# One tile more between the scores and the values of a causal attention, with a fourth buffer

## The reference

```python
xn = layernorm(x)
s = attn(xn, H=16, causal)        # Dh = 64: softmax(q k^T / 8, causal) v, then Wo, then layernorm
nodes = {-1: xn}
for c in range(6):                # a graph of 6 nodes
    q = ew[c,0] * (nodes[c-1] @ We[eq]);  k = ew[c,1] * (nodes[snode] @ We[ek])
    v = ew[c,2] * (nodes[snode + nsrc//2] @ We[ev])
    nodes[c] = act_w[c] * mha(q, k, v, H=8) + q      # Dh = 128, not causal
g = silu(layernorm(nodes[5]))
out = x + s * g
```

## Time and profile before

| what | value |
|---|---|
| runs shown | 8005.43 and 8122.02 us, median 8063.72 us |
| the profiled execution's own time | 7821.7 us |
| its span (slowest core, core 5) | 7820.2 us |
| spans of the 8 cores | 7784.9 to 7820.2 us |
| mean granted TensorE clock of the cores | 0.844 to 0.847 |
| PE busy, whole span | 5836.1 us (75%) |
| ACT busy | 2739.9 us (35%) |
| DVE busy | 2197.2 us (28%) |

### The profile page before, as it was taken

How to read it: one execution, slowest core, us unless ns; L and a number is a source line. 1 busy time by engine, 2 the same in 40 slices (tenths; PEclk the granted TensorE clock), 3 DMA queues, 4 the chain that set the end, 5 groups by cost and what they waited for, 6 DMA issues and landing times.

```text
span 7820.2 us, 62342 instructions; the slowest of 8 cores (7784.9 to 7820.2 us)
## 1 busy us (share of the span) xinstructions
PE 5836.1 (75%) x21827; PEld 1920.4 (25%) x21827; DVE 2197.2 (28%) x3068; ACT 2739.9 (35%) x2612; POOL 364.9 (5%) x354
## 2 busy tenths in 40 slices
PE   0677787777987779877789777897777878778830
PEld 0222233222332223322234222342222311111110
DVE  3133321333213332133321333213332122222155
ACT  0155432544215543155421455214552123333301
POOL 0100011000110001100011000110000100000000
PEclk9989998898998989989999888998888955566655
DMA  2300042000420004300033000230003200000013
GB/s 74 105 1 0 1 108 65 1 1 20 116 80 1 1 10 111 95 1 1 1 81 113 0 1 1 81 105 9 1 0 83 63 0 0 0 0 0 2 44 105
DMA packets 204568, 289.37 MB, mean 37 GB/s; under 512 B 141576, under 2 KB 141800, under 8 KB 204268
## 3 DMA queue, kind: packets, MB, share of 16 engines
q1 hardware_dynamic: 204236, 285.39, 12.7%
q0 software_dynamic: 32, 0.00, 0.0%
HBM read 218.24 MB, written 33.55 MB: 32 GB/s over the span
## 4 chain that ended last, share of the span: by engine, by line
PE 67%; DVE 18%; issue 6%; DMA 4%; ACT 4%; SPq 1%; DVEq 1%; POOL 0%; ACTq 0%; POOLq 0%
PE ps L384 17%; PE ps L564 9%; PE ps L869 8%; DVE attb L615 6%; PE ps L625 6%; PE ps L634 5%; PE ps L447 5%; PE ps L610 5%; DVE stat L515 4%; PE ps L508 3%; PE ps L595 3%; PE ps L586 3%; DVE attb L499 2%; DMA fio<-x 2%; ACT attb L675 1%
## 5 line engine op out<-in xcount | busy, mean ns | idle before, releaser
L675 ACT ACTIVATE attb<-ps,negM,scal 128x1024 bf16<-128x1024 f32 x1536 | 1770.0, 1201 | 1928.3 <-DVE negM L531 1432.9
L384 PE MATMUL ps<-slot,wbuf 128*128 128x512 bf16 x6144 | 1376.1, 385 | 227.4 <-POOL wbuf L358 202.4
L564 PE MATMUL ps<-qbuf,kbuf 128*128 128x512 bf16 x3072 | 1028.8, 426 | 172.4 <-ACT attb L675 148.8
L615 DVE TENSOR_TENSOR attb<-attb 128x1024 bf16<-128x1024 bf16 x768 | 536.1, 698 | 1788.2 <-PE ps L610 1770.0
L384 PEld LDWEIGHTS ps<-slot,wbuf 128*128 128x128 bf16 x6144 | 606.6, 99 | 980.9 <-issue 298.9
L869 PE MATMUL ps<-slot,wbuf 128*128 128x512 bf16 x3072 | 691.4, 384 | 85.1 <-POOL wbuf L358 85.1
L625 PE MATMUL ps<-attb,ones_bf 128*1 128x512 bf16 x1536 | 477.8, 393 | 359.4 <-DVE attb L615 353.0
L508 PE MATMUL ps<-attb,ones_sq 128*128 128x512 bf16 (+1 forms) x512 | 237.5, 562 | 610.0 <-DVE attb L499 608.8
L358 POOL CAST wbuf<-wstage 128x1024 bf16<-128x1024 f32 x344 | 363.2, 1060 | 5758.9 <-DVE kbuf L880 3656.9
L675 ACT ACTIVATE attb<-ps,negM 128x1024 bf16<-128x1024 f32 (+7 forms) x384 | 328.7, 864 | 686.3 <-PE ps L564 684.7
L610 PE MATMUL ps<-attb,slot 128*128 128x512 bf16 x1536 | 494.0, 406 | 16.5 <-DVE slot L737 16.5
(11 more groups left out here) (101 smaller groups left out, 2534.5 us busy)
## 6 DMA issues: line engine op xcount, KB each, us to landing
wstage<-fWe SPq DMA_DIRECT2D x120, 512.0 KB, 4.3
wstage<-fWv SPq DMA_DIRECT2D x48, 512.0 KB, 4.2
wstage<-fWq SPq DMA_DIRECT2D x48, 512.0 KB, 4.2
wstage<-fWk SPq DMA_DIRECT2D x48, 512.0 KB, 4.3
wstage<-fWo SPq DMA_DIRECT2D x48, 512.0 KB, 4.3
slot<-n_sp SPq DMA_DIRECT2D x40, 512.0 KB, 9.1
fio<-x SPq DMA_DIRECT2D x32, 512.0 KB, 4.1
n_sp<-slot SPq DMA_DIRECT2D x32, 512.0 KB, 2.6
```

The source lines that it names most:

```text
L384: t.matmul(ps[pb][:, sg * SEG:(sg + 1) * SEG], wtile(ws, kc, do * 128, 128), fchunk(ss, kc, th * TW + sg * SEG, SEG), start=(kc == 0), sto ...
L564: t_s = P.op("tensor", lambda t, kc=kc, sg=sg, pb=pb: t.matmul(ps[pb][:, sg * PSEG:(sg + 1) * PSEG], kf_tile_fn(kc), q_rhs_fn(sg * PSEG, P ...
L615: t_pr = P.op("vector", lambda v, a0=a0, a1=a1: v.tensor_tensor(attb[a0][:, 0:PW], attb[a0][:, 0:PW], attb[a1][:, 0:PW], ALU.add), waits=[ ...
L675: off=off: s.activation(attb[ab][:, off:PW], ps[pb][:, off:PW], AF.Exp, bias=negM[:, nc_:nc_ + 1], scale=scale_col),
```

## The change

Outside pair mode the probability tiles go round four buffers in place of three, and the row sums and values of a tile are emitted once four tiles are queued, in place of three. So they come after the scores of three later tiles, in place of two. The computation, the number of instructions and their sizes stay the same; three tiles, in place of two, are left to be emitted behind the loop.

```diff
--- before.py
+++ after.py
@@ -669,7 +669,7 @@
                 stash[0]()
                 stash[0] = None
             pb = j % 2
-            ab = j % (4 if pair_mode else 3)
+            ab = j % 4
             off = diag_off.get(kc, 0) if diag_off is not None else 0
             t_x = P.op("scalar", lambda s, pb=pb, ab=ab, nc_=negM_col,
                        off=off: s.activation(
@@ -689,7 +689,7 @@
             ready_q.append((j, ab, t_ready, off))
             if pair_mode and len(ready_q) >= 4:
                 stash[0] = pair_a(ready_q.pop(0), ready_q.pop(0))
-            elif not pair_mode and len(ready_q) >= 3:
+            elif not pair_mode and len(ready_q) >= 4:
                 jj, aa, rr, oo = ready_q.pop(0)
                 emit_lav(jj, aa, rr, off=oo, l_first=(jj == 0),
                          l_last=(jj == n_kc - 1), av_first=(jj == 0),
```

## The result

The changed kernel takes 1.0039 times the time of the one before (95% interval 1.0024 to 1.0054). Its profiled execution took 7822.53 us. The medians of all executions are 7971.81 us after and 7852.4 us before, in 15 and 14 executions; they hold executions in which one die ran at a lower clock throughout, which the ratio leaves out. Measured against a limit of 2% the two kernels are the same, as forecast, but the sign is the other one: the forecast factor was 0.9973.

The account below looks back on a forecast made before the run. PE, busy 75% of the span, was taken as the bound, with 33.8 us of waits open to the change. 9.1 + 13.2 - 1.2 = 21.1 us off 7821.7 gave 0.9973, carried to 8042 us, range 7980 to 8105.

Parts of the forecast that it names:

- The end of query tile 0: Last row sum's wait for L686: tile 4's work covers it, 11.5 us shrink to 2.4, gain 9.1 us.
- The start of query tile 1: Scores 3 ahead of row sum 0 cover the waits for L732, L737 and the mask: gain 13.2 us.
- What the step adds: Scores 3 need the buffer that the exp of tile 1 reads: 1.2 us of new wait, bounded by 16 us.
- the 9.1 us of scores 2 stay: Scores of tile 2 wait for the exp of tile 0 (L564 for L675) in 17 places, claimed unchanged at 9.1 us.
- L508's and L723's as before: PE's waits at the chain ahead of each head (L508, 139.8 us) and at L723, claimed unchanged.
- The clock: Rise near each head's end: moving it one tile is worth 1.29 us a head; taken as zero, 21 us either side.
- The sum: Whole kernel: 9.1 + 13.2 - 1.2 = 21.1 us off 7821.7 us, so 7800.6 us, factor 0.9973.
- The level: Whole kernel: factor 0.9973 applied to 8063.72 us gives 8042 us; level known to 58 us.
- the first: First tiles of query tile 0: the clock loses its rises, 5.9 us slower, 8070 us; chance 0.10.
- The second rival: Every query tile: scores 3 wait for the exp of tile 1, 16 us, so 6.3 us faster, 8057 us; chance 0.08.
- The third: Tiles behind each head's last scores: the clock rises one tile earlier, 41.7 us faster, 8021 us; chance 0.17.
- The extreme in it: Causal stage: closed gaps lift the clock throughout, at most 395 us off, some 7650 us; chance 0.03.

Follow-up runs that it names:

- the clock held low: Causal row sums and values contract only 64 of 128 key rows, in the kernel before and in the changed one: 7923.79 and 7892.76 us.
- start and end together: Against the kernel before: four buffers, tiles 0 and 1 in a row after scores 3, four tiles behind the last scores, old order between. Ratio 0.9803.
- pairs: Against the kernel before: four buffers, two scores then row sums and values of two tiles, throughout the causal attention. Ratio 0.9822.

## Why the prediction was wrong, step by step

- **The end of query tile 0: right.** Forecast 2.4 us in 5 places, measured 2.3 in 5 on the slowest core. The 0.5 us each are the working's; that there are again five is luck, since the rises moved: on the six cores with heads of 71.7 us there are one or two.
- **The start of query tile 1: right.** L732, L737 and the mask behind it are gone, 13.2 us. Only where the clock was high for most of the stage (128 rows) are 3.4 us of L737 and L682 left.
- **What the step adds: the term is right, a wait beside it was put at nothing.** Scores 3 were to wait 1.2 us, and waited 1.6 in seven places on the slowest core, with the clock held low never. But "the 9.1 us of scores 2 stay, since nothing in front of them changes" failed: the waits of L564 rose to 16.8 us in 39 places, and 6.1 of these 7.7 us are scores 2 waiting for the exp of tile 0 where query tile 1 begins at the high clock (16 places instead of 1). With the clock held low they did not rise (7.5 us in 15 places, against 8.1 in 16). On the six cores with heads of 71.7 us L564 grew by less than 3 us.
- **"L508's and L723's as before": wrong for L723.** Plus 12.0 us on the slowest core, where PE comes to it at the high clock (0.87 us in the timeline above), and within 2 us on the six other cores. At the fixed low clock it is 22.0 us in both orders.
- **The clock: this step failed.** "I take zero, and keep 21 us on both sides." On the slowest core PE was busy for 22.3 us more, in the median of the cores for 18.1 (887.5 to 905.6), and over the executions of the table the mean granted clock of a core fell from 0.8480 to 0.8444. The step asked whether the rise at each head's end moves by one tile. The rises in query tile 0 are what moved: on six cores they nearly went, on two they came at its end, where PE waits for ScalarE. With the order changed in two more places (start and end together) the clock was worth 159 us of PE's busy time. A bound of one tile a head was no bound, since it came from the rises that the trace had and not from what could change them.
- **The sum.** Of 21.1 us forecast the waits gave 22.6. Two new waits took 19.7 and the busy time 22.3: 19.7 + 22.3 - 22.6 = 19.4 us, against the 19.6 by which the stage grew on the slowest core. This is not the ratio's 30 us: the ratio compares other executions, and in the two profiled ones the rest of the span took 18.7 of the 19.6 us back.
- **The level.** The forecast of 8042 us came from two executions around 8063.72; fourteen give a median of 7852.4. The profiled execution's 7821.7 us was the better base.

Of the rivals the first came nearest: rises in query tile 0 were lost, and it was slower. Its price was too small. It set 30.6 us of lost high clock against all 21.1 us of gain and came to 5.9 us; the ratio makes some 30 us. It knew one core's five rises in query tile 0, while cores with short spans have more of them to lose, and it had no growth of the waits at L723 and L564. Its sign, a stage clock under 0.57, did not come (0.59 on the slowest core before and after). That core 2's loss is 30.6 us too is chance, it is another set of stretches. The second rival, scores 3 waiting for the exp of tile 1 everywhere, falls: there are seven such waits, and none with the clock held low. The sign set for it, 32 or more waits of L564, came all the same (39), because the view counts scores 2 and scores 3 together. The third had the right lever and the wrong handle. The extreme in it, a high clock in most of the stage, was to take at most 395 us off PE's work, and filling the rows, with the changed order, took off 247 (887.5 to 640.2); but what lifted the clock was not closed gaps. The rule of the Trainium skill quoted in the prediction (TensorE: Matmul & The Clock Gate, "What's actually happening"), by which recent busy-ness releases the throttle, fails here in its plain reading: 34.10 us without a gap stayed at 0.50, and so did 1211 us at 84% busy with 64-row matmuls. With 128-row matmuls less busy time (74%) had 0.82.

**What stays open.** Where exactly a rise comes was not derived, neither before nor after; the runs show which orders have more of them. The patterns also seem to hang on when the stage starts: after the change the time from the clock's last fall to the stage's first scores was 38.28 to 38.32 us on the cores with 1074.4, 38.47 to 38.53 on those with 1084.5, and 38.19 and 35.40 on the two long ones. No run set this time, so it is a reading and not shown. The kernel of start and end differs from the change in two places, and they were not run apart from each other. Why the stretches outside the stage differ by some 30 us between cores is open as well.

## What to carry to other kernels

If a stage has no gaps and a granted clock of about half, don't count waits first: look at how many rows its matmuls contract. Filling 64 rows up to 128 with zeros cost 1.9 us of an idle engine per head and took 2.4% off this kernel, 3.1% together with the changed order, where the change that removed 22 us of short waits came out 0.4% slower. When an order on PE is changed at such a clock, price the clock by an experiment, and read all cores and several executions: the profile of the slowest core had neither the short patterns of before nor a reason for the long ones of after, and the two profiled times were equal within 0.8 us.

## What was not expected of the hardware

- Rows, not busy time, held the clock down. With 64-row matmuls alone it stayed at 0.50 for the whole stage on eight cores; with 128-row matmuls it was 0.82 to 0.85 at the same number of matmuls and columns, and zeros in the added rows did as well as data (stage 853.4 and 853.8 us). A pair takes the same time either way (0.61 and 0.60 us at the high clock).
- Cores with the same program settle into different repeating head lengths, in the changed kernel 71.7 us in every head or 75.2, 75.2, 71.5 to the end of the stage; in the kernel before core 6 changed over to 64.7, 64.7, 72.0 on the way. With the clock held low, or with pairs, all eight cores agree within 3 us.
- A high clock can come where it is of little use: 3.50 us with PE busy for 2.22, and the waits that it opens (L723 from 16 to 31, L564 from 17 to 39) take back 1.28 us of the 1.8 (2.22 x 0.8) that it saves there.
